# A decoder layer on one core: the last 64 rows of its down product, spread over both halves of the partitions

## The reference, cut to what matters

```python
def _act_quant(x):
    scale = 127.0 / jnp.clip(jnp.max(jnp.abs(x), axis=-1, keepdims=True), EPS)
    return jnp.clip(jnp.round(x * scale), -128.0, 127.0) / scale
def _weight_quant(w):
    scale = jnp.clip(jnp.mean(jnp.abs(w)), EPS)
    return jnp.clip(jnp.round(w / scale), -1.0, 1.0) * scale
gate = silu(bitlinear(x, w_gate))      # x: 16 x 128 tokens x 1024;  w_gate, w_up: 2752 x 1024
up = bitlinear(x, w_up)
out = bitlinear(gate * up, w_down)     # w_down: 1024 x 2752
x = layernorm(x + out)
```

## Time and profile before

| | us |
|---|---|
| median of three runs | 1465.19 |
| the profiled execution, its own time | 1463.32 |
| its span in the trace | 1461.4 |
| PE busy | 1382.8 (95%) |
| DVE busy | 1068.1 (73%) |
| ACT busy | 613.3 (42%) |
| one turn of the second phase | 35.10 |
| matmuls of the down product (line 655), in all | 704 |
| granted clock of PE, mean | 0.979 |

### The profile page before, as it was taken

How to read it: one execution, slowest core, us unless ns; L and a number is a source line. 1 busy time by engine, 2 the same in 40 slices (tenths; PEclk the granted TensorE clock), 3 DMA queues, 4 the chain that set the end, 5 groups by cost and what they waited for, 6 DMA issues and landing times.

```text
span 1461.4 us, 23278 instructions
## 1 busy us (share of the span) xinstructions
PE 1382.8 (95%) x7576; PEld 695.5 (48%) x7576; DVE 1068.1 (73%) x1846; ACT 613.3 (42%) x1203; POOL 231.6 (16%) x270
## 2 busy tenths in 40 slices
PE   6787999999989999999999969999999999999996
PEld 2343555555545555554554544444444444444443
DVE  2886554555477787777877577888888888888884
ACT  4765654555455455445545342222222222222221
POOL 0112121212112221321322311000000000000000
PEclk9898999999999999999999979999999999999999
DMA  9502635454434534444443177222222222222200
GB/s 367 211 14 103 208 128 176 130 191 140 157 118 140 176 117 163 144 143 157 141 172 116 49 250 180 85 74 72 75 83 72 72 72 72 72 72 72 72 19 24
DMA packets 63570, 178.91 MB, mean 122 GB/s; under 512 B 15360, under 2 KB 26672, under 8 KB 63536
## 3 DMA queue, kind: packets, MB, share of 16 engines
q1 hardware_dynamic: 63536, 178.48, 37.5%
HBM read 153.02 MB, written 25.43 MB: 122 GB/s over the span
## 4 chain that ended last, share of the span: by engine, by line
PE 44%; issue 42%; DVE 5%; POOL 3%; ACT 2%; DMA 2%; SPq 1%; POOLq 0%; ACTq 0%; DVEq 0%
PE ps L484 36%; PE ps L475 3%; PE ps L576 2%; PE ps L558 2%; DMA ctx<-ctx 1%; POOL q L1324 1%; ACT tern L831 1%; DVE weights L1024 1%; PE ps L533 1%; ACT prob L753 1%; POOL rstd L1319 1%; DVE weights L1023 1%; DVE negmax L1058 0%; DVE prob L1069 0%; SPq L363 0%
## 5 line engine op out<-in xcount | busy, mean ns | idle before, releaser
L484 PE MATMUL ps<-weights,xT 128*128 128x512 f16 x2160 | 484.6, 381 | 0.0
L484 PEld LDWEIGHTS ps<-weights,xT 128*128 128x128 f16 x2160 | 209.7, 98 | 242.4 <-issue 9.8
L629 PE MATMUL ps<-weights 128*128 128x512 fp8e4 (+1 forms) x1536 | 300.0, 357 | 0.9 <-issue 0.9
L629 PEld LDWEIGHTS ps<-weights 128*128 128x128 bf16 x1536 | 146.7, 98 | 156.0 <-issue 1.4
L484 PE MATMUL ps<-weights 128*128 128x512 f16 x768 | 171.6, 384 | 7.6 <-issue 6.2
L851 ACT ACTIVATE weights<-ps,xscale 128x512 f32<-128x512 f32 x96 | 61.7, 643 | 249.2 <-PE ps L629 249.2
L655 PE MATMUL ps<-weights 128*128 128x512 fp8e4 x704 | 157.3, 380 | 0.0
L753 ACT ACTIVATE prob<-prob,negmax,undo 128x128 f32<-128x128 f32 x256 | 122.7, 482 | 20.7 <-DVE negmax L1060 20.7
L484 PEld LDWEIGHTS ps<-weights 128*128 128x128 f16 x768 | 75.7, 99 | 100.5 <-issue 10.7
L655 PEld LDWEIGHTS ps<-weights 128*128 128x128 bf16 x704 | 67.7, 98 | 76.0 <-issue 0.5
L1319 POOL TENSOR_TENSOR rstd<-rstd,expo 128x1 f32<-128x1 f32 x32 | 17.3, 541 | 535.9 <-DVE rstd L953 535.9
(11 more groups left out here) (145 smaller groups left out, 1836.9 us busy)
## 6 DMA issues: line engine op xcount, KB each, us to landing
wch<-w_ffn SPq DMA_DIRECT2D x96, 688.0 KB, 4.3
wch<-sim_scratch SPq DMA_DIRECT2D x96, 128.0 KB
ternary_scratch<-tern SPq DMA_DIRECT2D x48, 172.0 KB, 1.9
ctx<-ctx SPq DMA_DIRECT2D x16, 512.0 KB
weights<-x SPq DMA_DIRECT2D x16, 512.0 KB, 10.5
x_scratch<-weights SPq DMA_DIRECT2D x16, 512.0 KB, 2.9
weights<-x_scratch SPq DMA_DIRECT2D x16, 512.0 KB, 3.3
out<-k SPq DMA_DIRECT2D x16, 512.0 KB, 2.7
```

Source lines behind the costliest of these rows:

```text
L484: ins = nc.tensor.matmul(ps[:, bank], partsT[:, a, t], weights[:, t, w, half * HALF:(half + 1) * HALF], start=(t == 0 and a + w == 0), sto ...
L629: ins = nc.tensor.matmul(ps[:, 2 * w + a, 0:n], xqT[:, t], w8m[:, t, at:at + n], start=(t == 0), stop=(t == KT - 1))
```

## The change

The last tile is no longer padded. Its two column halves now lie on the two halves of the partitions: rows 0 to 63 of a new buffer `down_tail` (bf16, 128 x 512) hold columns 0 to 511 of the last 64 weight rows, rows 64 to 127 hold columns 512 to 1023. Two transfers bring them in fp8 and VectorE converts them once, in turn 0. The last 64 columns of `hq` are transposed twice, into partitions 0 to 63 and into partitions 64 to 127 of the bank. The two matmuls of t = 21 then use 64 rows each: c = 0 the upper half of the array's rows, c = 1 the lower. Both memsets and the semaphore `padded` go; a semaphore `tail_ready` comes.

```diff
+TAIL = I - (IT - 1) * P
+        down_tail = over(over_out, HALF // 2).bitcast(BF16)
 # SP
-                    sp.dma_start(down8[0:I - full, IT - 1].bitcast(U8), src[full:I]).then_inc(ffn_in, 16)
+                    for c in range(2):
+                        sp.dma_start(down8[c * TAIL:(c + 1) * TAIL, IT - 1, 0:HALF].bitcast(U8),
+                                     src[full:I, c * HALF:(c + 1) * HALF]).then_inc(ffn_in, 16)
 # PE
-                if isinstance(i, int) and i == 0:
-                    pe.wait_ge(padded, 1)
-                    for t in range(lo, hi):
+                    for t in range(lo, min(hi, IT - 1)):
                         ins = nc.tensor.transpose(bank[:, (t - lo) * P:(t - lo + 1) * P], hq[:, t * P:(t + 1) * P], idb[:])
+                    if hi == IT:
+                        for c in range(2):
+                            ins = nc.tensor.transpose(bank[c * TAIL:(c + 1) * TAIL, (hi - 1 - lo) * P:(hi - lo) * P],
+                                                      hq[:, (IT - 1) * P:I], idb[:])
+                if isinstance(i, int) and i == 0:
+                    pe.wait_ge(tail_ready, 1)
-                        ins = nc.tensor.matmul(ps[:, AC + c], hT[:, t], down8[:, t, c * HALF:(c + 1) * HALF],
+                        rows = slice(0, P) if t < IT - 1 else slice(c * TAIL, (c + 1) * TAIL)
+                        ins = nc.tensor.matmul(ps[:, AC + c], hT[rows, t],
+                                               down8[:, t, c * HALF:(c + 1) * HALF] if t < IT - 1 else down_tail[rows],
                                                start=(t == 0), stop=(t == IT - 1))
-            pe.wait_ge(ffn_in, 16 * 8)
+            pe.wait_ge(ffn_in, 16 * 9)
 # DVE, between the last row maximum and the scale
+                if isinstance(i, int) and i == 0:
+                    dve.wait_ge(ffn_in, 16 * 9)
+                    nc.vector.tensor_copy(down_tail, down8[:, IT - 1, 0:HALF]).then_inc(tail_ready, 1)
 # POOL
-                    st.wait(st.done(nc.gpsimd.memset(down8[64:P, IT - 1], 0.0)))
-            pool.wait_ge(pj_full[1], pj_out(B - 1) + 1)
-            nc.gpsimd.memset(hq[:, I:IT * P], 0.0).then_inc(padded, 1)
```

More of the change, by code:

```diff
@@ L255, in decoder @@
         set_up2 = sem("set_up2")
-        padded = sem("padded")
         x1_loaded = sem("x1_loaded")
@@ L271, in decoder @@
         h_rounded = sem("h_rounded")
+        tail_ready = sem("tail_ready")
         hq_ready = sem("hq_ready")
```

## The result

| | before | changed |
|---|---|---|
| median, us (13 runs each, side by side) | 1466.29 (1463.82 to 1468.58) | 1469.79 (1466.96 to 1471.59) |
| ratio | | 1.0025, 95% interval 1.0016 to 1.0033 |
| span of the profiled execution | 1461.4 | 1466.4 |
| one turn of the second phase, mean of 14 | 35.10 | 35.33 |

A forecast was written before the change was run, and what follows sets the result against it. PE, busy 95% of the span, was taken as the bound. Turns +3.75, turn 15 +0.27 and conversion +0.48 made +4.5 on a 1465.19 us median: 1469.7 us, bounds 1468.7 to 1471.5, stated range 1467.4 to 1472.0.

The forecast's parts named there:

- A switch costs 0.095 in either direction: On PE, changing between the full array and halves of it costs 0.095 us each way; read from f32 rows.
- Rival 1: Switching costs nothing in bf16, so the kernel is not slower: -0.18 us a turn, 1462.8 us; chance 0.08.
- The pair runs beside itself: Two matmuls on different halves of the array's rows cost as much as one, saving 0.22 us a turn.
- Rival 3: The matmul pair does not run beside itself at 512 columns: +0.21 us more a turn, 1472.9 us; chance 0.06.
- The down product's end: Last full matmul to the next gate matmul: the pair's gain is eaten by two switches, +0.01 us a turn.
- The transposes' end: Last transpose batch to first down matmul: doubled transpose with two switches, +0.24 us a turn (0.22 to 0.26).
- Rival 2: Only the matmul pair pays for switches, the transposes' are hidden or lacking: +0.06 us a turn, 1466.6; chance 0.09.
- Turn: Each second-phase turn, on PE's gapless stretch: +0.25 us (0.22 to 0.35), or +3.75 over 15 turns.
- The conversion: VectorE's tail conversion in turn 0, between last maximum and scale, counts in full: +0.48 us (0.15 to 0.57).
- The second transfer: Two tail transfers for one before the second phase: 1.6 us of cover, so 0 us (0 to 1.5).
- Rival 4: The second tail transfer lands late, 1.5 us more: 1471.2 us; chance 0.05.
- Turn 15: Last turn, transposes at granted clock 0.50 (+0.36 us), its end -0.09: together +0.27 us (0.1 to 0.4).

The follow-up runs named there:

- t_split: Changed kernel with the full transpose of t = 20 put between the two 64-column transposes, four switches there instead of two; 35.60 us a turn.
- serial64: Changed kernel with both column halves of the tail on rows 0 to 63, one 64-column transpose, two matmuls on the same array half; 35.54 us a turn.
- t_only: Kernel before with two 64-column transposes in place of the last one, full matmuls over zero-padded weights kept; 35.33 us a turn.
- t_moved: Changed kernel with the two 64-column transposes moved from the end of the last batch to the end of the third; 35.144 us a turn.
- dma_split: Kernel before with only the tail's transfer issued as two column halves; turns 35.11 us, last output product to end of span 7.66 us.
- sp_short: Changed kernel with the 21 full down tiles brought in by two transfers instead of three; turns 35.33 us, end stretch 8.62 us.
- m_only: Changed kernel with its full-shape transposes over zero padding put back, only the two 64-row matmuls of t = 21 kept; 35.10 us a turn.
- conv_act: Changed kernel with its conversion on ScalarE instead of VectorE; turn 0 35.31 us instead of 35.53, end stretch 7.65 us.
- conv_only: Kernel before with a conversion of the padded tail added on VectorE in turn 0, into an unread buffer; turn 0 35.85 us, end stretch 7.65 us.

## Why the prediction was right

The prediction held: in direction, in size (+4.5 said, +3.5 between the medians, and an interval of 2.3 to 4.8 us), and in its steps. That its 1469.7 lies so near the measured median of 1469.79 is luck: it was added to 1465.19, and over the 13 runs the median before is 1466.29.

*A switch costs 0.095 in either direction, in bf16 too.* This was carried over from f32 rows. t_split shows it by itself: two more switches, a lost overlap and two loads made 0.27; less 0.05 for the overlap and 0.02 to 0.04 for the loads, that is 0.09 to 0.10 a switch. In the changed kernel the start of the small transposes is 0.149 behind the fourth full one (1164.50 in the timeline; 0.056 + 0.093). Rival 1 fell. One count behind the 0.095 was loose: of the other shape, column halves, the trace of before has 30 places behind line 484 and not 31; 22 follow at 0.31, two at 0.34, and six later still.

*The pair runs beside itself.* serial64: 0.20 us a turn when it can't. Rival 3 fell.

*The down product's end: +0.01 said, -0.003 measured.* 0.312 + 0.003 + 0.318 + 0.011 = 0.644 against 0.647. I took 0.02 for the load, and it is 0.007.

*The transposes' end: +0.24 said, +0.23 measured* (t_only 35.33), with a load of 0.024 where I took 0.03. By the Trainium skill, "TensorE: Matmul & The Clock Gate", LDWEIGHTS, a load of 64 columns alone would take about 0.053 us, an estimate from the page's formula; less than that shows in the matmul's length, 0.024. Rival 2, that the transposes' switches are hidden, was false for the place where the change put them, and nearly true at another: t_moved pays 0.04 of the 0.23.

*Turn:* +0.25 said, +0.233 measured, times 15 = 3.5.

*The conversion: +0.48 said, +0.21 measured.* This is the term that was mis-sized. The slope between two rows gave 0.48 for an instruction that is 0.42 long, and "it counts in full" was the wrong half: it stands behind an instruction for whose result the next one must wait, and half of it falls into that wait. The wait could have been read in the trace of before, as 0.39 between two starts.

*The second transfer:* no cost said. PE's first gate product came at 891.76 instead of 891.42 in the profiled execution, and dma_split and sp_short leave the turns as they are. The two were issued in 3.07 and 0.59 us, the second at 879.50, and each landed 9.1 to 9.2 us behind its issue: both were there by 888.7, 3 us ahead of that product. Rival 4 did not come in. The 0.34 is no sign of it: the first phase alone moves this start by more.

*Turn 15:* +0.27 said. In the profiled executions it is +0.04 up to the last output product (1457.78 - 1421.95 = 35.83, against 35.79). But this stretch was 35.8 to 37.7 us in the other traces, by how long the low clock lasts, so its own cost can't be told.

*Not foreseen:* +0.93 at the very end, from the last output transfer. The sum that the traces give is 3.5 + 0.21 + 0.04 + 0.93 = 4.7, and 0.34 from the start: the 5.0 between the two spans. That this total meets the forecast of 4.5 so closely is partly luck: the conversion was put 0.27 too high, turn 15 0.23 and the turns 0.25, and the missing end of 0.93 made up for them. The medians differ by only 3.5, what the 15 turns alone give, so whether the other executions have that end too is not shown.

## What to carry to other kernels

Working beside each other on halves of the array pays only when enough is done between the switches: here one switch in and one out cost 0.19 us, and one saved 512-column matmul is 0.217. Before splitting a tile, find in the trace what the way into and out of such a stretch costs, and count it for every place, the transposes that prepare the layout included; they may have nothing to gain. A switch, like any product that is ready, costs little where the engine waits, and that wait was worth more to the plain kernel (0.18 us a turn) than the split was.

## What the runs showed that I had not expected

The last output transfer landed in 3.6 us and not 2.6 in six of the twelve traces (the changed kernel, m_only, t_split, serial64, t_moved, sp_short), so that the end came 0.93 to 0.96 us later. In all six one 8 KB packet of the instruction queue starts near the end of the transfer; in the changed kernel it starts at 1464.52 and takes 0.31. All but two of the 128 data packets are under way or done by then; these two, of 4 KB each, start only when it has ended, at 1464.83 and 1465.18. DMA view of the changed kernel from 1464.75 to 1465.9:

```profile
DMA  0070000000000060000000000000000000000000
...
q1 hardware_dynamic: 3, 0.01, 3.7%
```

In the kernel before no packet at all falls between 1460.7 and the end of the span. The other six traces have the instruction packet before or behind the transfer. All six slow ones have the changed kernel's conversion on VectorE and its altered PE code, and conv_act shows that moving the conversion away suffices to end it. Which engine's fetch it is, and why conv_only doesn't have it, stays open.

In turn 15 PE is idle for 4.4 us ahead of the transposes, and the granted clock then falls to 0.50, the 1.2 GHz level. How long it stays there varies: in four traces it is back at 1.00 after a stretch like the first below, and from the last turn's first gate product to the last output product it takes 35.8 to 36.1 us; in the other eight it lasts through two such stretches, and it takes 36.4 to 37.7. Busy time by stretch, with the granted clock behind POOL, the changed kernel and then m_only:

```profile
1445.00:1448.40 3.40, 3.25 (x24) 2.25 (x25) 2.73 (x6) 0.00 (x0) 0.00 (x0) 0.50 0.00 0
1448.40:1457.00 8.60, 8.60 (x41) 3.89 (x40) 0.22 (x1) 0.00 (x0) 0.00 (x0) 1.00 0.01 2
```

```profile
1440.80:1444.20 3.40, 2.37 (x20) 1.94 (x21) 3.02 (x8) 0.64 (x1) 0.00 (x0) 0.50 0.03 5
1444.20:1447.60 3.40, 3.40 (x12) 1.39 (x11) 0.80 (x2) 0.00 (x0) 0.00 (x0) 0.50 0.00 0
```

In m_only PE ran at the low level for both stretches though it was busy through the second, and from the last turn's first gate product to the last output product it took 36.96 us, against 35.83. The traces differ at two more places: the second phase starts at 887.6 to 893.7 us, and its turn 0 takes 34.9 to 36.7 us at a granted clock of 1.00, more than the edits account for; why stays open. The runs of one kernel differ by nearly 5 us, more than the change itself, so the turns of the loop, which repeat to 0.01 us, had to carry the argument.
